# Seven-product feed-forward stage: earlier first-block operands, other buffers for the first set, low parts and loads in a new order

## What is computed

```python
xq, ctx = layer_norm(x), layer_norm(context)
q, k, v = xq @ q_w, ctx @ kv_w (keys), ctx @ kv_w (values)      # 16 heads of 32
x = x + softmax(where(mask, -max, q k^T * scale)) v @ proj_w + proj_b
h = layer_norm(x)
return x + gelu(h @ fc1_w + fc1_b) @ fc2_w + fc2_b              # 512 -> 2048 -> 512
```

## Time and profile before

| | |
|---|---|
| median of 3 runs | 1142.0 us (1138.11 to 1142.04) |
| time of the profiled execution | 1137.7 us |
| its span, first to last instruction | 1135.9 us |
| TensorE matmul busy | 1079.0 us, 95% |
| VectorE busy | 829.3 us, 73% |
| ScalarE busy | 513.7 us, 45% |
| GpSimd busy | 323.3 us, 28% |
| mean granted TensorE clock | 0.988 of full |

### The profile page before, as it was taken

The page is one execution under the profiler, slowest core; times in us unless marked ns, Lnnn a source line. Parts: engine busy times, 40 slices in busy tenths (PEclk is TensorE's granted clock), DMA queues, the critical chain, the costliest instruction groups (busy, mean ns, idle before and its releaser), DMA issues.

```text
span 1135.9 us, 16876 instructions
## 1 busy us (share of the span) xinstructions
PE 1079.0 (95%) x5665; PEld 904.7 (80%) x5665; DVE 829.3 (73%) x1469; ACT 513.7 (45%) x1326; POOL 323.3 (28%) x243
## 2 busy tenths in 40 slices
PE   8999999999999776999989999999999999999998
PEld 7798999899999655777768777787777788788887
DVE  8887888888887857767788667668656658656655
ACT  4665566655666625444533333344233335323221
POOL 3335534554446737222430400030400030400000
PEclk9999999999999997999989999999999999999999
DMA  7111121112110137555465643433753433833421
GB/s 246 17 46 38 56 85 48 49 49 77 64 48 20 56 114 283 167 193 197 163 217 181 238 165 121 176 139 130 249 220 122 176 109 132 300 143 119 161 74 74
DMA packets 54746, 149.46 MB, mean 132 GB/s; under 512 B 13269, under 2 KB 21501, under 8 KB 46487
## 3 DMA queue, kind: packets, MB, share of 16 engines
q1 hardware_dynamic: 54095, 147.56, 36.5%
q10 hardware_dynamic: 584, 1.06, 0.3%
HBM read 108.13 MB, written 39.85 MB: 130 GB/s over the span
## 4 chain that ended last, share of the span: by engine, by line
PE 72%; DVE 18%; issue 3%; ACT 2%; DMA 2%; POOL 1%; SPq 1%; DVEq 0%; ACTq 0%
PE bank L1735 24%; PE bank L1765 24%; PE bank L1613 8%; PE bank L1571 6%; PE bank L1552 3%; DVE gT L1384 3%; PE bank L1602 3%; DVE acc L1392 2%; PE bank L1744 2%; DVE xTl L1135 2%; DVE PTl L1152 1%; PE bank L1584 1%; DVE nmax L1129 1%; DVE hbn L1357 1%; DVE w1r L1347 1%
## 5 line engine op out<-in xcount | busy, mean ns | idle before, releaser
L1765 PE MATMUL bank<-w2r,gT 128*128 128x512 f32 x1536 | 371.8, 396 | 17.5 <-DVE acc L1392 17.5
L1765 PEld LDWEIGHTS bank<-w2r,gT 128*128 128x128 f32 x1536 | 284.8, 189 | 92.1 <-DVE acc L1392 34.8
L1735 PE MATMUL bank<-hop,w1r 128*128 128x512 f32 x1344 | 313.3, 391 | 16.5 <-DVE ybuf L1379 16.3
L1735 PEld LDWEIGHTS bank<-hop,w1r 128*128 128x128 f32 x1344 | 253.4, 189 | 70.3 <-issue 17.3
L1392 DVE TENSOR_TENSOR acc<-bank,acc 128x512 f32<-128x512 f32 x256 | 175.1, 688 | 102.3 <-PE bank L1765 100.5
L1379 DVE TENSOR_TENSOR ybuf<-bank,ybuf 128x512 f32<-128x512 f32 x224 | 145.2, 684 | 79.5 <-PE bank L1735 78.8
L1007 ACT ACTIVATE ybuf<-ybuf,cols 128x512 f32<-128x512 f32 x128 | 91.7, 716 | 157.3 <-DVE ybuf L1379 157.3
L1384 DVE TENSOR_TENSOR gT<-ybuf,gT 128x512 fp32r<-128x512 f32 x128 | 101.4, 812 | 54.0 <-ACT gT L1011 52.6
L841 ACT ACTIVATE S<-S,nmax 128x77 f32<-128x77 f32 x256 | 88.8, 353 | 47.0 <-DVE nmax L1129 47.0
L1000 ACT ACTIVATE ybuf<-bank 128x512 f32<-128x512 f32 x32 | 19.2, 598 | 180.2 <-PE bank L1735 179.6
L735 POOL TENSOR_TENSOR acc<-acc,fc2b 128x512 f32<-128x512 f32 x32 | 43.7, 1383 | 154.5 <-DMA acc<-x_scratch 154.3
(11 more groups left out here) (112 smaller groups left out, 1652.1 us busy)
## 6 DMA issues: line engine op xcount, KB each, us to landing
w1r<-w_scratch SPq DMA_DIRECT2D x24, 1792.0 KB, 7.4
w2r<-w_scratch SPq DMA_DIRECT2D x24, 1024.0 KB, 5.1
w_scratch<-w1r SPq DMA_DIRECT2D x8, 1792.0 KB, 7.0
xr<-in_x SPq DMA_DIRECT2D x16, 512.0 KB, 3.6
x_scratch<-xr SPq DMA_DIRECT2D x16, 512.0 KB, 2.8
hring<-x_scratch SPq DMA_DIRECT2D x32, 256.0 KB, 3.1
acc<-x_scratch SPq DMA_DIRECT2D x32, 256.0 KB, 4.3
w_scratch<-w2r SPq DMA_DIRECT2D x8, 1024.0 KB, 4.9
```

Source lines behind the costliest of these rows:

```text
L1735: mm = pe.matmul(bank_[:, :], w1r[:, w1_slot(s), c, w, kk * P:(kk + 1) * P], hop[i][:, d, kk, :], start=(kk == 0 and n == 0), stop=(kk == ...
L1765: mm = pe.matmul(bY[t % 2][:, :], gT[s % 2][:, j, d, t * P:(t + 1) * P], w2r[:, s % 2, j, w, :], start=(n == 0), stop=(n == 5))
```

## The change

1. The norms and transposes of block 0's rows go from attention steps 6 to 13 to steps 4 to 11. `w1_sums(0)` goes to step 11, `hop_T` of block 0 to steps 12 (T1, T3) and 13 (T2, T4), from steps 13, 14 and 15.
2. In steps 14 and 15 several high and low parts change place. `gelu` of the first quarter of set 0 is done in step 15.
3. For block 0, set 0, other buffers are used: `ybuf[3]` and the bias lie in T2, the raw second weights in T1, so that they need not wait for the store of the last attention unit. C12 now comes before C22 in `y_add` and in `GS`.
4. SyncE's order at the crossing from attention to feed-forward, and in block 0, is new.
5. On VectorE in every block `g_lo` 2 and 3 of set s-1 come at the head of set s, `g_lo` 0 and 1 between the `acc_add`, and `h_stats` ahead of the additions; `w1_lo` is spread. `h_T` of a set's second tile comes after fc2 tile 7 instead of 6.
6. `load_w1(b, 2)` comes after the loop of output stores and accumulator loads. `hop_T` of the next block comes first in set 6 on GpSimd.

```diff
-    NORM2 = {NU - 2 - BT + t: t for t in range(BT)}
-    LOOP = (0, NU - 2 - BT)
+    NORM2 = {NU - 4 - BT + t: t for t in range(BT)}
+    LOOP = (0, NU - 4 - BT)
...
+    def y_of(b, s, n):
+        return T2[:, 0, :] if isinstance(b, int) and b == 0 and s == 0 and n == 3 else ybuf[n][:, :]
+    def w2_in(s):
+        return T1 if s == 0 else w2raw
+    def bias2(b):
+        return T2[:, 1, :] if isinstance(b, int) and b == 0 else fc2b[:, :]
...
         def load_w2raw(s):
-            p_w2.wait(sp, 0, s - 1)
+            if s == 0:
+                v_hop.wait(sp, 0, 2)
+                p_T.wait(sp, 0, 2)
+            elif s == 1:
+                sp.wait_ge(d_x2st, 16 * NU)
+            else:
+                p_w2.wait(sp, 0, s - 1)
...
         for t in range(BT):
             load_acc(0, t)
-        sp.wait_ge(d_x2st, 16 * NU)
-        load_w2raw(0)
-        sp.dma_start(fc2b[:, :], ...)
-        store_w1(0)
-        store_w1(1)
+        step(last_unit, more=False)
         def block(b, before, first=False, last=False):
             for s in range(SETS):
+                if first and s == 0:
+                    load_w1raw(2)
+                    load_w2raw(1)
+                    load_fc2b(1)
+                    store_w1(1)
                 if not last and s == 0:
                     load_h(b + 1, 0)
                     load_h(b + 1, 1)
...
-                        if t == 1:
-                            load_w1(b, 2)
                         if t >= 2:
                             sp.wait_ge(d_out[t - 2], b * 16)
                             load_acc(b, t - 2)
+                    load_w1(b, 2)
...
             for s in range(SETS):
+                if not last and s == SETS - 2:
+                    hop_T(b + 1, range(4))
...
-            if isinstance(b, int) and b == 0 and s == 0 and i == C22:
+            if isinstance(b, int) and b == 0 and s == 1 and i == C22:
                 dve.wait_ge(d_x2st, 16 * NU)
...
+                if s > 0:
+                    g_lo(b, s - 1, 2)
+                    g_lo(b, s - 1, 3)
                 if not (first and s == 0):
                     y_add(b, s, C11)
...
+                if made:
+                    w1_lo(s + 1, 0)
+                    w1_lo(s + 1, 1)
...
                 add(s, 7)
+                if last and s == SETS - 1:
+                    g_lo(b, s, 2)
+                    g_lo(b, s, 3)
...
-                    if t == 6 and len(tiles) > 1:
+                    if t == 7 and len(tiles) > 1:
                         h_T(b + 1, tiles[1])
```

More of the change, by code:

```diff
@@ L1017, in block @@
                 refill = not last and s == SETS - 1
+                made = first and 0 < s < SETS - 1
                 if first and s == 0:
@@ L1025, in block @@
                     hop_hi(b + 1, 0)
-                gelu(b, s, 0)
+                if not (first and s == 0):
+                    gelu(b, s, 0)
                 if refill:
@@ L1334, in step @@
             if tail == 2:
+                hop_lo(0, 6)
                 w1_lo(1, 2)
@@ L1406, in block @@
                 tiles = () if last else TILES.get(s, ())
+                made = first and 0 < s < SETS - 1
+                if not first and s == 0:
+                    hop_lo(b, 6)
+                if s > 0:
+                    g_lo(b, s - 1, 2)
+                    g_lo(b, s - 1, 3)
                 if not (first and s == 0):
@@ L1456, in block @@
                 add(s, 2)
-                if first and 0 < s < SETS - 1:
-                    w1_lo(s + 1, 0)
-                    w1_lo(s + 1, 1)
+                g_lo(b, s, 1)
                 add(s, 3)
```

207 lines of the change are left out of this document (111 added, 96 removed).

## The result

The changed kernel takes 1109.8 us (median of 4 runs, 1108.4 to 1111.26). The kernel before, run beside it, takes 1141.6. The ratio is 0.9728, 95% interval 0.9703 to 0.9754: 2.7% faster. The prediction was 1103. The profiled execution took 1111.26 us, its span is 1109.5. TensorE is busy for 1072.7 us (97% of the span, before 95%), VectorE for 832.3 (75%).

The account below looks back on a forecast made before the run. TensorE, busy 95% of the span, bounds the kernel, so only its gaps can be won; 7.5+3.5+7.7+6.3+5.5+5.8+1.7-2.1 = 35.9 us off 1137.7 gives 1101.8, moved up to 1103. Range 1090 to 1117, main forecast 1094 to 1110 at 64%.

Parts of the forecast that it names:

- Crossing: From E, the end of attention's last projection, to set 2's start: 38.85 us, gain 7.5, new gap 10.5.
- Rival 1: The new gap at the row tile does not come or is under 3 us: 1090, chance 17%.
- Attention: Attention steps 4 to 15 together: gain 3.5 us, bounds 1 to 6.
- Step 14: Attention step 14: the 3.34 us gap and 1.5 of half clock go, about 0.9 comes back; gain 3.9 us.
- step 15: Attention step 15: opening products wait 1.8 us for low parts; about 3.0 lost instead of 2.6, loss 0.4.
- steps 4 to 13: I take 0: Attention steps 4 to 13: row tiles move by two steps, nothing is added; 0 us, bounds -1.5 to +1.5.
- sign of no gap over 2 us: Attention steps 14 and 15: the changed profile should show no gap over 2 us.
- Sets: Feed-forward sets: 21.15 us with one tile, 21.75 with two; gains 7.7, 6.3, 5.5, 5.8 and 1.7.
- Sets 6 and 7: Block 0, sets 6 and 7: 49.83 to 43.5 us, gain 6.3, TensorE waiting about 1.7.
- The end: Last set: two `g_lo` come behind set 6's last `acc_add`, so the last fc2 starts later; loss 2.1 us.
- Rival 2: Waits go on elsewhere: sets with row tiles keep 0.85 each, or block 0 its contention; 1116, chance 15%.
- Rival 3: Slower than before: `load_w1(b, 2)`, behind the output and accumulator loop, lands late for set 2; chance 2%.

Follow-up runs that it names:

- run 1: Changed kernel with the second block's two rows fetched ahead of the eight accumulator fetches: 1106.0 us, 0.9711 of the kernel before.
- run 2: Changed kernel with VectorE's additions ahead of row statistics and weights' low parts in set 1 of block 0: 1102.6 us, 0.9668 of before.
- run 4: Changed kernel with the edits of run 1 and run 2, but the first set's fourth result in its old home: 1107.5 us, 0.9715 of before.
- run 6: Changed kernel with all four of GpSimd's `hop_T` operand sums of block 0 in attention step 13, none in step 12: 1106.9 us.
- run 7: Changed kernel with the first `hop_lo` and `w1_lo` placed earlier on VectorE at the end of attention step 14: 1105.2 us, 0.9700 of before.
- run 11: Changed kernel with run 1, run 5, run 6, run 7, a variant of run 2 and 96 bytes free behind the masks: 1090.6 us.
- run 9: Kernel before with only the mask buffers moved ahead of the projection weights, shifting the buffers behind by 1568 bytes: 1145.7 us, 1.0065 of before.
- run 12: Kernel of run 11 with the row's normalization earlier on VectorE and 480 bytes free behind the masks instead of 96: 1083.3 us, 0.9481 of before.
- run 5: Changed kernel with later gelu low parts back between the first accumulator additions in the last block's last set: 1107.8 us, 0.9722 of before.

## Why the prediction was right, and where it wasn't

The forecast was 1103 and the range 1090 to 1117; 1109.8 lies in it, on the slow side, and at the very edge of the 1094 to 1110 of the main forecast. Against the profiled execution of before the sum promised 35.9 us, and the profiled execution after gave 1137.7 - 1111.26 = 26.4. Of the 9.5 us that are missing, 5.5 are those of attention. By its own steps:

- **Crossing**: 38.85 us predicted, 39.55 measured. The mechanism was right: the gap at the third tile of fc2 (10.5 predicted, 11.53 measured), held by `h_stats`, held by its transfer (E+20 predicted, 438.70 - 416.64 = E+22.1 measured), and half clock behind it (4.57 us for 2.9, 1.7 lost; 2.3 predicted). Rival 1 falls. What the count hid is that the row was not the only bar: run 1 shows that without it 6.1 us stay, close to the 7 that the text gave as its lower bound, and run 2 that the order on VectorE mattered more.
- **Homes**: the other buffers of the first set were priced nowhere by themselves. The place of the fourth result is worth 6.9 us once the gap is gone (run 4); that of the raw second weights was not undone by itself. That in the changed kernel all of the 6.9 lay under the gap is likely, but no run shows it.
- **Attention**: the step that failed. 3.5 us of gain predicted, with bounds of 1 to 6; measured -2.04 (the end of attention moved from 414.60 to 416.64), of which 0.7 is a later first projection. Step 14 went as said (3.5 us less, 3.9 predicted), step 15 nearly (0.65 more, 0.4 predicted). What failed is "steps 4 to 13: I take 0", with -1.5 to +1.5 as bounds: they took 237.5 us instead of 233.4, 4.1 more. There I asked only whether `hop_T` would hold back GpSimd's own chain, not what VectorE does at that moment. In step 12 it normalizes, and those two operations became 3.16 us. Step 12 took 24.95, run 6 gives 22.77. Half clock behind it cost 1.5 more in step 13. Step 11, where `w1_sums` now stands, took 0.45 more; no run tells why. In run 6 steps 4 to 13 take 233.8, 0.4 more than before. The earlier trace rows shows such a hold, for operations with two operands in SBUF, and I did not ask for it in the place where the work went. The wait in step 15 was foreseen at 1.8 us and came at 2.2, against my own sign of no gap over 2 us there; the half clock behind it wasn't foreseen. Runs 6 and 7 give more than all of it back: with both edits, in run 11, attention ends at 407.75.
- **Sets**: 85.8, 43.5, 169.3, 170.5 and 143.9 predicted; 86.10, 44.86, 169.83, 170.45 and 144.81 measured. That looks exact and is luck. The sets were to get faster by losing waits, at the pitch of before. They lost more than I counted (a set with none had two late matmuls of its own, 0.14 us together, and one tile costs 0.57, not 0.6), and most paid 0.27 us each for a slower pitch, for which the sum had no term: the moved masks stood in the code of the change, and I gave them no price. Two errors, of some 0.2 us a set one way and 0.27 the other, nearly cancelled. Runs 9 and 12 separate them: at the old pitch the same set takes 20.40 us, and one with a row tile 20.97, where I wrote 21.15.
- **Sets 6 and 7**: the gap of 1.7 us beside `hop_T` was there (1.58), and 1.4 us more was lost around it (44.86 for 43.5). It isn't the pitch's: at the old pitch, in run 12, the two sets take 44.88. What it is was not tried.
- **The end**: 2.1 predicted, 2.03 measured, and run 5 takes it away.
- Rivals 2 and 3 did not come: the waits of the sets are gone, and the late `load_w1(b, 2)` is never waited for.

## What to carry to other kernels

Before you move GpSimd work into idle time, look at what VectorE does in that very stretch: an operation that reads SBUF beside it can be held for the whole of GpSimd's, in this case even with one operand (3.16 us for two beside it, 1.00 without). Put an instruction that waits for a transfer behind those on its engine that don't, and fetch small, early wanted rows ahead of large ones; here the order was worth more than the fetch. After any edit of the memory plan compare the mean duration of one unchanged product: 7 ns in each of 1344 were 8 us, more than any of the repairs but that of the crossing.

## What the runs showed of the hardware

- The place of buffers in SBUF changes TensorE's pace, and most likely it is that of the weights. With the input weights at the old place, or 2048 bytes above it, products are 0.2267 us apart; 1568 bytes above it 0.2332, 1600 above 0.2334, 1664 above 0.2324. Starting at a multiple of 64 or of 128 bytes doesn't bring it back. The products' other operands did not move. By the kernels' memory plans the weights start a multiple of 512 bytes from `hop` in both fast places, and 32, 64 and 128 bytes past one in the three slow ones. Whether it is the place within 2048 bytes, within a smaller unit that divides it (512 is one), or relative to another buffer is open; no run tells them apart.
- `tensor_scalar` with one operand in SBUF was held by GpSimd in two places: 3.16 us for two beside `hop_T` and 1.00 without, 2.72 for one beside `w2_lo` and 0.61 in run 12.
- The clock behind a short gap isn't the same each time. Behind the gap of 2.3 us in step 12 the granted clock of the next 4 us was low (0.57 to 0.69) in five traces of nine and full in four. Behind the gap of 2.2 us that opens step 15 it was low (0.57 to 0.59) in all nine traces that have it. Step 12 in the changed kernel and in run 1:

```profile
345.78:349.78 4.00, 4.00 (x11) 3.14 (x12) 1.98 (x5) 1.23 (x1) 4.00 (x2) 0.57 0.00 0
```

```profile
345.23:349.23 4.00, 4.00 (x17) 3.28 (x18) 1.97 (x5) 1.24 (x1) 4.00 (x2) 1.00 0.00 0
```

  0.57 is most of the 4 us at 1.2 GHz, 1.00 all of it at 2.4; the work ahead was the same. It makes 1.5 us of difference in step 13 (24.01 and 22.45), so single profiled executions can't be compared to a microsecond across such a gap.
